# One picture's gray value: three engines or VectorE alone, in a one-core ViT tower with mixture of experts

## The reference

```
gray  = 0.2989*x[:,0] + 0.587*x[:,1] + 0.114*x[:,2]       # 8 x 256 x 256
edge  = (|conv(gray, sx)| + |conv(gray, sx.T)|) / 2        # 3x3 Scharr taps
h     = layernorm(edge + causal_attention(edge))           # one head, D = 256
out   = layernorm(h + mixture_of_8_experts(h))             # top-1, capacity 320, 256->1024->256
```

## Time and profile before

| | |
|---|---|
| median of 3 runs | 251.41 us (251.34 to 252.23) |
| the profiled execution | 251.09 us, of which the span is 249.3 us |
| PE busy | 232.7 us, 93% of the span |
| PEld busy | 223.1 us, 89% |
| DVE busy | 183.8 us, 74% |
| ACT busy | 151.6 us, 61% |
| POOL busy | 98.1 us, 39% |
| TensorE clock granted, mean | 0.987 of full speed |
| chain that ended last, share of the span | PE 75%, DMA 5%, DVE 5%, issue 5%, POOL 5%, ACT 2% |

### The profile page before, as it was taken

The page is one execution under the profiler, slowest core; times in us unless marked ns, Lnnn a source line. Parts: engine busy times, 40 slices in busy tenths (PEclk is TensorE's granted clock), DMA queues, the critical chain, the costliest instruction groups (busy, mean ns, idle before and its releaser), DMA issues.

```text
span 249.3 us, 4995 instructions
## 1 busy us (share of the span) xinstructions
PE 232.7 (93%) x1673; PEld 223.1 (89%) x1673; DVE 183.8 (74%) x557; ACT 151.6 (61%) x354; POOL 98.1 (39%) x169
## 2 busy tenths in 40 slices
PE   6999999999999999878799999999999999999940
PEld 5899999999999998647799999999999999999940
DVE  4885697887979799786456796749967678779540
ACT  5336567787877786465665477656775758656100
POOL 7000227584665658438100020156260332513662
PEclk9999999999999999999999999999999999999995
DMA  5939563174896020201499919257092460100100
GB/s 175 289 100 304 137 206 135 38 233 148 246 378 224 2 83 15 68 0 43 118 338 293 383 56 313 68 164 261 0 300 93 140 229 3 45 2 24 35 4 0
DMA packets 28378, 35.48 MB, mean 142 GB/s; under 512 B 2780, under 2 KB 25291, under 8 KB 28354
## 3 DMA queue, kind: packets, MB, share of 16 engines
q1 hardware_dynamic: 26144, 31.71, 39.9%
q0 software_dynamic: 1792, 3.47, 3.9%
q10 hardware_dynamic: 418, 0.00, 0.1%
HBM read 26.97 MB, written 9.47 MB: 146 GB/s over the span
## 4 chain that ended last, share of the span: by engine, by line
PE 75%; DMA 5%; DVE 5%; issue 5%; POOL 5%; ACT 2%; POOLq 1%; ACTq 0%; SPq 0%; DVEq 0%
PE bank L1274 14%; PE bank L1276 14%; PE bank L1275 14%; PE bank L1345 14%; PE bank L1399 4%; PE bank L1362 4%; POOL out_dram L573 3%; DMA bqc<-in_L_attn_bq_dram 2%; PE bank L1524 2%; DMA dispatched<-trow,slot 2%; PE bank L1574 2%; PE bank L1415 1%; PE bank L1373 1%; PE bank L1417 1%; PE bank L1416 1%
## 5 line engine op out<-in xcount | busy, mean ns | idle before, releaser
L1191 DVE SCALAR_TENSOR_TENSOR h_lo<-bank,h_hi 128x320 fp32r<-128x320 f32 x58 | 28.3, 488 | 27.4 <-ACT h_hi L817 24.8
L817 ACT ACTIVATE h_hi<-bank 128x320 fp32r<-128x320 f32 x58 | 25.3, 436 | 35.4 <-PE bank L1276 35.4
L573 POOL DMA_INDIRECT out_dram<-tokens_mem,images x24 | 28.0, 1168 | 37.9 <-ACT tokens_mem L834 17.1
L1274 PE MATMUL bank<-einT_hi,w_hi 128*128 128x320 f32 x128 | 40.6, 317 | 0.6 <-DVE einT_lo L1183 0.3
L1275 PE MATMUL bank<-einT_lo,w_hi 128*128 128x320 f32 x128 | 39.5, 308 | 0.0
L1276 PE MATMUL bank<-einT_hi,w_lo 128*128 128x320 f32 x128 | 39.5, 308 | 0.0
L947 DVE TENSOR_TENSOR w_lo<-w_raw,w_hi 128x1024 fp32r<-128x1024 f32 x32 | 38.8, 1214 | 0.0
L1274 PE MATMUL bank<-h_hi,w_hi 128*128 128x320 f32 x112 | 35.2, 314 | 0.1
L1276 PE MATMUL bank<-h_hi,w_lo 128*128 128x320 f32 x112 | 34.6, 309 | 0.0
L1275 PE MATMUL bank<-h_lo,w_hi 128*128 128x320 f32 x112 | 34.6, 309 | 0.0
L745 ACT ACTIVATE w_hi<-w_raw 128x1024 fp32r<-128x1024 f32 x32 | 33.7, 1052 | 0.0
(11 more groups left out here) (231 smaller groups left out, 577.3 us busy)
## 6 DMA issues: line engine op xcount, KB each, us to landing
w_raw<-in_L_ffn_W_dram SPq DMA_DIRECT2D x16, 1024.0 KB, 7.8
images<-in_x_dram SPq DMA_DIRECT2D x7, 768.0 KB, 4.8
dispatched<-blank SPq DMA_DIRECT2D x4, 645.0 KB, 8.6
images<-dispatched SPq DMA_DIRECT2D x9, 258.0 KB, 7.2
out_dram<-lone SPq DMA_DIRECT2D x8, 256.0 KB, 7.6
images<-in_x_dram SPq DMA_DIRECT2D x2, 384.0 KB, 5.1
images<-dispatched SPq DMA_DIRECT2D x9, 64.5 KB, 7.1
out_dram<-tokens_mem,images POOLq DMA_INDIRECT x24, 2.5
```

The lines of the kernel that those rows point to most:

```text
L573: pool.indirect_dma_start(out_rows, bass.IndirectOffsetOnAxis(ap=ein[0:n, e, j, D + 1:D + 2].bitcast(U32), axis=0), z[0:n, e % 2, j, :], N ...
L817: act.activation(hidden_halves(n)[0], bank[n % 2][:, 0:CAP], ACT.Relu).then_inc(h_hi_ready, 1)
L1191: dve.scalar_tensor_tensor(lo, bank[n % 2][:, 0:CAP], 0.0, hi.bitcast(F32), ALU.max, ALU.subtract).then_inc(h_ready, 1)
L1274: pe.matmul(to, ah, bh, start=first, stop=False)
```

## The change

The sum of red, green and blue of pictures 2 to 7 is made by `make_gray`: two scalar_tensor_tensor instructions of VectorE, the second of which waits until the first is complete. The scaling of blue on ACT and the addition on POOL go, as do the two semaphores between the three engines. `gray_ready` is raised by VectorE.

```diff
@@ POOL
-            def add_blue(b):
-                pool.wait_ge(blue_ready, b - 1)
-                pool.wait_ge(warm_ready, b - 1)
-                pool.tensor_tensor(red[:, b % 2], red[:, b % 2], pix[:, b % 2, 2], ALU.add).then_inc(gray_ready, 1)
...
-                if i + 2 < B:
-                    add_blue(i + 2)
@@ ACT
-            def scale_blue(b):
-                act.wait_ge(pix_in[b % 2], 16 * (b // 2 + 1))
-                act.activation(pix[:, b % 2, 2], pix[:, b % 2, 2], ACT.Copy, scale=GRAY[2] / GRAY[0]
-                               ).then_inc(blue_ready, 1)
...
-                if i + 2 < B:
-                    scale_blue(i + 2)
-                elif i < L:
+                if i == L - 1:
                     split_high(0)
@@ DVE
-            def red_and_green(b):
-                dve.wait_ge(pix_in[b % 2], 16 * (b // 2 + 1))
-                dve.scalar_tensor_tensor(red[:, b % 2], pix[:, b % 2, 1], GRAY[1] / GRAY[0], pix[:, b % 2, 0],
-                                         ALU.mult, ALU.add).then_inc(warm_ready, 1)
...
                 if i + 2 < B:
-                    red_and_green(i + 2)
+                    make_gray(i + 2)
                 else:
                     split_low(0)
```

More of the change, by code:

```diff
@@ L237, in vit_tower_kernel @@
         early_turned = sem("early_turned")
-        blue_ready = sem("blue_ready")
-        warm_ready = sem("warm_ready")
         wr_centred = sem("wr_centred")
```

## The result

The changed kernel takes 255.82 us (median of 4 runs, 255.58 to 256.12), the kernel before 251.58 us beside it (4 runs). The ratio is 1.017, 95% interval 1.0153 to 1.0188: slower by 1.7%, where no change was predicted. The profiled execution took 256.12 us, its span 254.4 us instead of 249.3; the mean clock granted to TensorE is 0.976 instead of 0.987.

The account below looks back on a forecast made before the run. PE was taken to bound the loop, other engines mattering only where it waits. Savings of 0.06 us from 251.09 gave 251.03, and 0.32 for the runs' median 251.35 us, no measurable change; range 250.7 to 252.3.

Parts of the forecast that it names:

- my rivals: Slower through POOL holding DVE (0.06), slower through DVE being late (within the first case), faster through hidden PE waits (0.05).
- The slower one: In the loop, POOL's small instructions beside the gray pair delay DVE's tokens, 0.28 us in five passes: 252.8 us, chance 0.06.
- the list at the prediction's end: Signs expected in the changed profile: PE passes of 11.18 us, DVE's spacings and idle times, unstretched tokens, engines' busy totals.
- the spare time: DVE's margin before half 1 waits for `edges`: 0.12 us in pass 3, 0.31 in pass 1, near 0.2 in others.
- a sign that it is wrong: In the loop, DVE no longer waiting for ACT's `edges` would show the prediction wrong.
- The cover: DVE's wait for `edges` before half 1 hides the added 0.71 us a pass; without it 4.3 us in all.
- the predicted -0.06 us: In PE's loop, unstretched tokens end the wait of `project_keys`: 0.04 us in one pass, 0.02 in another.
- Three totals: Busy times over the kernel: DVE up by 4.0 us, POOL down by 7.9, ACT down by 3.9.

Follow-up runs that it names:

- pad12: The changed kernel with 12 one-element memsets that compute nothing added to POOL's setup; 251.67 us, ratio 0.9995.
- before_pad116: The kernel before, its gray sum on three engines, with 116 one-element memsets added to POOL's setup; 255.8 us, ratio 1.016.
- fill: The changed kernel with ten unused matmuls of 512 columns on PE where it waits for the hidden half; 253.85 us, ratio 1.0076.
- reorder126: The changed kernel with scale_out(1) ahead of POOL's first output scatter and 126 one-element memsets in POOL's setup; 251.35 us, ratio 0.998.
- dvepad: The changed kernel with 4 one-element memsets on POOL and 20 on DVE in the setup; 251.2 us, ratio 0.9978.
- both: The changed kernel with scale_out(1) ahead of POOL's first output scatter and 20 one-element memsets on DVE; 250.79 us, ratio 0.9978.
- pad3: The changed kernel with 3 one-element memsets added to POOL's setup; 251.54 us, ratio 1.0004.
- pad4: The changed kernel with 4 one-element memsets added to POOL's setup; 251.35 us, ratio 0.9995.
- reorder: The changed kernel with scale_out(1) ahead of the first output scatter on POOL, no memsets; 251.68 us, ratio 1.0003.
- tail73: The changed kernel with 73 one-element memsets added to POOL's setup; 251.64 us, ratio 1.0002.

## Why the prediction was wrong

**What failed** is the step "The stages behind the loop hold none of the changed instructions. They shift with the loop's end and are not changed otherwise." It is true of the instructions, and false of the time. Twelve instructions fewer on POOL put a fetch of POOL's program at its first output scatter. That gave 2.96 us between two instructions that normally stand 0.55 apart, so 2.4 us; with the scatters behind it 0.2 us slower in sum and a start 0.46 earlier, 2.2 us of lateness went by `yrstd`, `ynmr`, ACT's queue and `h_lo` to PE, and the low clock behind PE's wait made it 4.2 us. pad12 shows that the loss goes when the count of instructions is restored, before_pad116 that the count alone makes it, fill parts wait and clock, reorder126 shows the way by which it costs. That the count works through a fetch of code is read from the packet in the pause and from the step of 128.

None of my rivals had this. The slower one (POOL's small instructions hold DVE) had the sign, but another place and mechanism, and it did not happen. The range's upper end of 252.3 lay 3.5 us too low.

**What held**, in the loop, by the list at the prediction's end. Rows of DVE's timeline, pass 3 (beside the earlier trace rows) and pass 0 (beside the earlier trace rows):

```profile
59.68 0.67 DVE L859 SCALAR_TENSOR_TENSOR red<-images 128x512 f32<-128x512 f32 x1
60.38 0.69 DVE L861 SCALAR_TENSOR_TENSOR red<-images,red 128x512 f32<-128x512 f32 x1
60.99 0.42 DVE L914 TENSOR_TENSOR xT<-tokens_mem 128x256 f32<-128x256 f32 x1
61.32 0.16 DVE L1047 RECIPROCAL trow<-lsum 128x2 f32<-128x2 f32 x1
61.40 0.40 DVE L914 TENSOR_TENSOR xT<-tokens_mem 128x256 f32<-128x256 f32 x1
...
25.33 0.42 DVE L914 TENSOR_TENSOR xT<-tokens_mem 128x256 f32<-128x256 f32 x1
```

- The pair is 0.70 us apart (predicted 0.71), the tokens 0.61 behind the second (0.59).
- No tokens instruction is stretched: 0.40 to 0.43 us, also in pass 0, where it was 1.44. What POOL's addition cost the tokens, 1.02 us in pass 0 and 0.18 in pass 3, is gone.
- DVE's idle time ahead of half 1 is 0.23 us in pass 1 (predicted 0.2 to 0.3), but 0.09, 0 and 0.03 in passes 2, 4 and 5, where the same was predicted. The prediction counted the spare time from 0.07 us behind the start of `factor`, the profile counts it from its end, 0.16 behind the start. In pass 3 it is zero instead of 0.1, because the pause of 0.46 us stands ahead of it; without that pause the pass is 11.19 us (dvepad). So in passes 3 and 4 DVE no longer waits for `edges`, which the prediction named as a sign that it is wrong; PE has no wait there, and pass 4 took 11.19 us. The cover was as thin as predicted or thinner, and it held.
- From pass 0 to pass 6 PE needs 67.26 us before (17.54 to 84.80), in the changed kernel 67.43 (17.36 to 84.79), in dvepad 67.22 (17.45 to 84.67) and in both 67.19 (18.05 to 85.24). So the predicted -0.06 us is there as -0.04 and -0.07, one trace each, and DVE's pause covered it with 0.2. Such a size can't be told in the time of a run.
- Three totals were mis-sized. DVE's busy time rose by 2.8 us, not 4.0, since the tokens no longer stretched give back 1.4. POOL's fell by 6.2, not 7.9: of `scale_lone`, L488 (L490 before) now takes 0.64 us instead of 0.19 in pass 3, beside DVE's gray sum. It is POOL that is held there, not DVE as in the slower rival. ACT's fell by 2.3, not 3.9: the records of the six scalings overlap those of ACT's neighbouring instructions, and taken out of the trace of before they lower its busy time by 2.6 only. None of these is on PE's path.
- The picture's load in pass 3 is issued 0.53 us earlier (61.10 instead of 61.63), not 0.75, because DVE was 0.22 late.

**What stays open.** The border costs 2.2 to 2.4 us ahead of the first output scatter, 0.3 ahead of a scatter of routed rows, and nothing in pad3, pad4, reorder and tail73. In the changed kernel and in before_pad116 it comes right behind a long wait of POOL, as if the next piece were asked for only when the wait had ended; in reorder126, where the pause is as long (2.73 us), two instructions of POOL stand between the wait's end at 162.49 and the pause, so the wait alone does not explain it. In all three the packet starts 1.1 to 1.3 us behind the first of the two small instructions, and POOL goes on only behind it. In before the packet is at 113.3, when POOL had already gone on at 113.1. Why POOL stands still for the packet in one case and not in the other is not known.

In pad3, pad4 and reorder the packet comes at about 119.6 us, at the start of POOL's long idle time, which hides it. That the wait and the fetch stand in this order is read from the traces; that it must be so was not tested by itself, nor was the 128 told from its neighbours other than by the two matches, 116 + 12 and 126 + 2, and by where the pauses stand (196th and 324th). That DVE's pause is a border rests on dvepad and both alone; in the changed kernel the packet nearest to it comes at 58.5 us, when the pause is over. The 0.46 us by which the changed kernel was ahead at 157 us was not followed either.

## What to carry to other kernels

A change that adds or removes instructions moves the fetch borders in all of its engine's program behind it; so a loss far behind the change, with a hole between two instructions that depend on nothing, is first tested with instructions that compute nothing, put in or taken out. Where an engine's queue holds first something long whose lateness no one minds (scatters) and then something short that the critical engine needs (a scale), turn them round: that took no instruction and made the pause harmless. And a wait of TensorE costs more than its length, when the clock falls behind it: here 2.2 us of lateness cost 4.2.

## What the runs showed of the hardware

- The engines' programs come in packets of their own queues. The profile counts 11 of them on q14 in the changed kernel, 0.09 MB, so 8 KB each, and 12 with 116 more instructions on POOL. They can't all be POOL's: at one packet for 128 instructions, the recorded ones of DVE (662), ACT (532) and POOL (264) make 5 + 4 + 2 = 11 (an estimate from the trace). At the border ahead of the first output scatter POOL stood still for 2.2 to 2.4 us more than normal, DVE at its own for about 0.4 us. The Trainium skill (Runtime: NRT & Kernel Launch, section "Instruction fetch mechanics") says that the sequencer fetches the next page while it executes the current one, in blocks of 256 instructions, and that the cost is mostly hidden. tail73, pad3 and pad4 agree with "mostly hidden"; the changed kernel and before_pad116 show 2.4 and 2.2 us that were not, and shifts by 128 instructions brought the same pause back, half the stated block.
- Behind 2.67 us in which PE waited, the granted clock was 0.50 for 6.2 us in the changed kernel's profiled execution, and in that of before_pad116, behind 2.7 us of the same wait, it stayed at 1.00. Filled with ten matmuls, so that 0.37 us were left, it stayed at 1.00 (fill).
- Beside DVE's instructions on 128x512 elements, a POOL instruction on two numbers per partition took 0.64 us instead of 0.19, while DVE's own took 0.67 and 0.69 as ever. With POOL's addition on 128x512 elements beside DVE's tokens on 128x256 it had been DVE that was held: 1.44 us instead of 0.42.
